# A gated delta-rule layer on one Trainium2 core: the triangular inverse kept in 32x32 blocks, a pipeline one turn deeper, three projection banks in rotation, a new order of steps

## The reference

```python
q = silu(conv4(x @ Wq)); k = silu(conv4(x @ Wk)) * 128**-0.5; v = silu(conv4(x @ Wv))
alpha, beta = sigmoid(x @ Wa + ba), sigmoid(x @ Wb + bb)
def step(S, (qt, kt, vt, at, bt)):               # for each of 2048 tokens, S is 128x128
    err = S @ kt - vt
    S = at * S - bt * outer(err, kt)
    return S, S @ qt
out = x + (layernorm(o) * ln_w + ln_b) * sigmoid(x @ Wg) @ Wo + experts
```

## Time and profile before

| | |
|---|---|
| median of 3 runs | 4384.37 us (4383.68 to 4387.27) |
| profiled execution, its own time | 4386.71 us |
| its span | 4385.1 us |
| PE busy in the span | 4174.3 us, 95% |
| DVE busy | 3028.0 us, 69% |
| ACT, POOL busy | 46%, 41% |
| granted TensorE clock, mean | 0.99 |

### The profile page before, as it was taken

How to read it: one execution, slowest core, us unless ns; L and a number is a source line. 1 busy time by engine, 2 the same in 40 slices (tenths; PEclk the granted TensorE clock), 3 DMA queues, 4 the chain that set the end, 5 groups by cost and what they waited for, 6 DMA issues and landing times. The chain is left out here.

```text
span 4385.1 us, 94472 instructions
## 1 busy us (share of the span) xinstructions
PE 4174.3 (95%) x28800; PEld 3435.8 (78%) x28800; DVE 3028.0 (69%) x7067; ACT 2033.0 (46%) x4992; POOL 1805.5 (41%) x3109
## 2 busy tenths in 40 slices
PE   8999799999999999999999999999999999996999
PEld 6777688888888788888888888888888888885887
DVE  4444577777777777777777777777777777774222
ACT  3433355555555555555555555555555555553111
POOL 3444444444444444444444444444444444441000
PEclk9999899999999999999999999999999999997999
DMA  3333411111111111111221111111111111113453
GB/s 128 131 139 139 151 38 40 39 39 39 39 41 39 39 39 39 39 39 39 77 77 39 39 39 40 40 39 39 40 39 39 39 39 39 39 27 104 147 145 114
DMA packets 371455, 270.27 MB, mean 62 GB/s; under 512 B 153456, under 2 KB 284528, under 8 KB 369360
## 3 DMA queue, kind: packets, MB, share of 16 engines
q1 hardware_dynamic: 368848, 261.29, 21.0%
q0 software_dynamic: 2560, 8.39, 0.5%
HBM read 209.85 MB, written 59.77 MB: 61 GB/s over the span
## 5 line engine op out<-in xcount | busy, mean ns | idle before, releaser
L1247 PE MATMUL bank<-hx_hi,w_hi 128*128 128x512 f32 x2048 | 927.4, 453 | 136.6 <-DVE conv L1052 110.1
L1247 PE MATMUL bank<-hx_lo,w_hi 128*128 128x512 f32 x2048 | 907.8, 443 | 0.0
L1247 PE MATMUL bank<-hx_hi,w_lo 128*128 128x512 f32 x2048 | 895.0, 437 | 0.0
L1052 DVE SCALAR_TENSOR_TENSOR conv<-bank,tap,conv 128x512 f32<-128x512 f32 x1152 | 848.7, 737 | 15.7 <-ACT conv L1190 6.4
L1247 PEld LDWEIGHTS bank<-hx_hi,w_hi 128*128 128x128 f32 x2048 | 390.6, 191 | 200.2 <-issue 82.4
L921 POOL TENSOR_TENSOR masked<-LT,mask 128x256 f32<-128x256 f32 x512 | 412.9, 837 | 190.8 <-DVE LT L1070 190.7
L1008 DVE SCALAR_TENSOR_TENSOR S<-S,gamma,bank 128x128 f32<-128x128 f32 x480 | 164.7, 343 | 449.5 <-PE bank L1333 447.2
L940 POOL TENSOR_TENSOR oG<-oT,gT 128x512 f32<-128x512 f32 x128 | 166.0, 1297 | 709.1 <-ACT oT L1208 709.1
L1247 PEld LDWEIGHTS bank<-hx_hi,w_lo 128*128 128x128 f32 x2048 | 390.0, 190 | 75.4 <-issue 43.8
L897 POOL TENSOR_TENSOR prods<-Lb,Tc 128x28 f32<-128x28 f32 (+6 forms) x896 | 204.0, 228 | 504.1 <-ACT Lb L1176 441.8
L1136 ACT ACTIVATE MT<-bank 128x256 f32<-128x256 f32 x512 | 196.3, 383 | 457.3 <-PE bank L1270 457.2
(11 more groups left out here) (147 smaller groups left out, 9529.6 us busy)
## 6 DMA issues: line engine op xcount, KB each, us to landing
gamma<-gamma_d SPq DMA_DIRECT2D x128, 258.0 KB, 3.2
alpha<-alpha_d SPq DMA_DIRECT2D x128, 256.0 KB, 3.6
oT_d<-oG SPq DMA_DIRECT2D x128, 256.0 KB, 2.4
o_raw<-oT_d SPq DMA_DIRECT2D x32, 1024.0 KB, 6.8
gu_raw<-in_gate_up SPq DMA_DIRECT2D x17, 1408.0 KB, 6.2
dn_raw<-in_down SPq DMA_DIRECT2D x17, 512.0 KB, 4.6
x_in<-in_x SPq DMA_DIRECT2D x8, 1024.0 KB, 9.3
w_raw<-in_Wk SPq DMA_DIRECT2D x32, 256.0 KB, 3.1
```

Source lines behind the costliest of these rows:

```text
L1052: dve.scalar_tensor_tensor(out=conv[i][:, to], in0=PJ[i][:], scalar=tap[:, i, j + 1:j + 2], in1=conv[i][:, to], op0=ALU.mult, op1=ALU.add) ...
L1247: last = pe.matmul(dst, a[:, i, k], b[:, k, cols], start=(j == 0), stop=(j == 3 * KC - 1))
```

## The change

The inverse up to 32x32 is held in compact form: `TTb` and `Tnb` keep, for each chunk, the four diagonal 32x32 blocks as 128 partitions x 32 columns. The merges to 16 and 32 become matmuls of 32x32 diagonal blocks (16 in each of four visits); the product is not masked beforehand on POOL, but afterwards on DVE, which writes `Yb` (new L1045) in place of ACT's copy `MT`. After the second level ACT puts the blocks in place in `TT` (L1169) and in `Tn64` (L1175). `diag` and `Lc` work on the diagonal blocks alone.

The inverse is split over two turns: `inv` (group g+2) does the two small levels, `late` (group g+1) the merges to 64 and 128, `AT`, and the rows of k and v. `proj` moves to group g+3, and there is one more turn ahead of the first full one. At four places of a turn (`VISIT_AT`) PE does the blocks of both groups behind each other, 16 of `inv`, then 8 or 4 of `late`. `AT`'s matmuls and DVE's `AT` are one piece instead of two. The projections rotate over banks 0, 1 and 2 (`PJ_OF`), with the wait for each looked up in `PJ_FREED`. A turn has 38 steps where it had 19, and all tables are new.

```diff
+TB = 32
 LEVELS = [8, 16]
-STEPS = 19
-CHAIN = {1: 0, 2: 1, 4: 2, 5: 3, 7: 4, 8: 5, 10: 6, 11: 7, 13: 8, 14: 9, 16: 10, 17: 11}
...
-MT_AT = {6: 0, 9: 1}
-TT_AT = {7: 0, 10: 1}
-Y32_AT, T32_AT, Y64_AT, T64_AT = 13, 14, 16, 17
...
+PJ_OF = [[0, 1, 2, 0], [1, 2, 0, 1], [2, 0, 1, 2], [0, 1, 2, 1]]
+PJ_FREED = [[(1, 0), (1, 3), (1, 2), (0, 0)], [(1, 1), (1, 2), (1, 3), (0, 0)],
+            [(1, 1), (1, 2), (1, 3), (0, 0)], [(1, 1), (1, 2), (1, 3), (0, 1)]]
...
+VISIT_AT = {9: 0, 15: 1, 28: 2, 34: 3}
...
+YB_AT = {11: 0, 28: 1}
+TT_AT = {19: 0, 31: 1}
...
+PLACE_AT = {8: (0, 1), 7: (2, 3)}
...
+        TTb = sb("TTb", [P, 2, G, TB])
+        Tnb = sb("Tnb", [P, 2, G, TB])
+        Yb = sb("Yb", [P, G, TB])
+        Tn64 = sb("Tn64", [2 * TB, G, 2 * TB])
+        MT = sb("MT", [P, G, 2 * TB])
+        TT = sb("TT", [P, 2, G, C])
...
-        masked = sb("masked", [P, len(LEVELS), G, C])
-        TT = sb("TT", [P, 2, G, C])
-        Tn = sb("Tn", [P, G, C])
...
-        PJ, IB, TR, CO = (bank[0], bank[1], bank[2], bank[1]), bank[3:5], bank[5], bank[6:8]
+        PJ, WL, WH, TR, CO = bank[0:3], bank[3], bank[4], bank[5], bank[6:8]
...
-            turn(eng, -1, 2, False, False, True, False)
-            turn(eng, -1, 3, False, True, True, False)
+            turn(eng, -1, 1, False, False, False, True, False)
+            turn(eng, -1, 2, False, False, True, True, False)
+            turn(eng, -1, 3, False, True, True, True, False)
             for g in range(GROUPS):
-                turn(eng, 0, g, True, True, True, g > 0)
+                turn(eng, 0, g, True, True, True, True, g > 0)
             with nc.Fori(1, NH - 1, engines=bass.OrderedEngineSet([eng.engine]), hint_back_edge=True) as hh:
                 for g in range(GROUPS):
-                    turn(eng, hh, g, True, True, True, True)
+                    turn(eng, hh, g, True, True, True, True, True)
             for g in range(GROUPS):
-                turn(eng, NH - 1, g, True, g < 3, g < 2, True)
-            turn(eng, NH, 0, False, False, False, True)
+                turn(eng, NH - 1, g, True, g < 3, g < 2, g < 1, True)
...
-                    if inv and s == 1:
-                        pool.wait_ge(solve_done, at(SOLVE_PER, 2))
-                        wait(pool, chain_done, at(12, 0))
-                        pool.tensor_tensor(TT[:, (g + 1) % 2].rearrange("p c (q t) -> p c q t", t=SB),
-                                           Tc[:].rearrange("p c (o t) -> p c o t", o=1).to_broadcast([P, G, P // SB, SB]),
-                                           same[:].rearrange("p (c q t) -> p c q t", c=1, t=SB)
-                                           .to_broadcast([P, G, P // SB, SB]), ALU.mult).then_inc(t8_done, 1)
-                    if proj and s in MASK_AT:
-                        lvl = MASK_AT[s]
-                        pool.wait_ge(lt_done, at(1, 3))
-                        for c in range(2):
-                            wait(pool, step_done[c], at(STEP_PER, 1, 2 * lvl + 2))
-                            pool.tensor_tensor(masked[:, lvl, half(c)], LT[:, g % 2, half(c)], mask[lvl][:], ALU.mult)\
-                                .then_inc(mask_done, 1)
...
+                    if inv and s == T8P_AT:
+                        pool.wait_ge(solve_done, at(SOLVE_PER, 3))
+                        wait(pool, late_done, at(LATE_PER, 1))
+                        wait(pool, placed, at(4, 1))
+                        pool.tensor_tensor(TTb[:, cur].rearrange("p c (q t) -> p c q t", t=SB),
+                                           Tc[:].rearrange("p c (o t) -> p c o t", o=1).to_broadcast([P, G, TB // SB, SB]),
+                                           same_c[:].rearrange("p (c q t) -> p c q t", c=1, t=SB)
+                                           .to_broadcast([P, G, TB // SB, SB]), ALU.mult).then_inc(t8_done, 1)
...
+                    if inv and s in YB_AT:
+                        l = YB_AT[s]
+                        dve.wait_ge(step_done, at(4, 2, 2 * l + 1))
+                        dve.tensor_tensor(Yb[:], WL[:, 0:G * TB].rearrange("p (c t) -> p c t", c=G),
+                                          mask_c[:, l].rearrange("p (c t) -> p c t", c=1).to_broadcast([P, G, TB]),
+                                          ALU.mult).then_inc(yb_done, 1)
+                    if inv and s in TT_AT:
+                        l = TT_AT[s]
+                        dve.wait_ge(step_done, at(4, 2, 2 * l + 2))
+                        dve.tensor_tensor(TTb[:, cur], TTb[:, cur], WL[:, 0:G * TB].rearrange("p (c t) -> p c t", c=G),
+                                          ALU.subtract).then_inc(tt_done, 1)
+                        dve.wait_ge(tt_done, at(2, 2, l + 1))
+                        dve.transpose(Tnb[:, cur], TTb[:, cur]).then_inc(tn_done, 1)
...
-                    if inv and s in TT_AT:
-                        lvl = TT_AT[s]
-                        for c in range(2):
-                            dve.wait_ge(step_done[c], at(STEP_PER, 1, 2 * lvl + 3))
-                            dve.tensor_tensor(TT[:, par, half(c)], TT[:, par, half(c)],
-                                              IB[c][:, 0:2 * C].rearrange("p (c t) -> p c t", c=2), ALU.subtract)\
-                               .then_inc(tt_done[c], 1)
-                        for c in range(2):
-                            dve.wait_ge(tt_done[c], at(len(LEVELS), 1, lvl + 1))
-                            dve.transpose(Tn[:, half(c)], TT[:, par, half(c)]).then_inc(tn_done[c], 1)
...
+                        wait(dve, lc_done, at(1, 3))
+                        for q in range(P // TB):
+                            dve.tensor_tensor(diag[quad(q)], LT[quad(q), (g + 3) % 4, :, quad(q)],
+                                              same_c[quad(q)].rearrange("p (c t) -> p c t", c=1).to_broadcast([TB, G, TB]),
+                                              ALU.mult).then_inc(diag_done, 1)
...
-                    if inv and s in MT_AT:
-                        lvl = MT_AT[s]
-                        for c in range(2):
-                            act.wait_ge(step_done[c], at(STEP_PER, 1, 2 * lvl + 2))
-                            act.activation(MT[:, half(c)], IB[c][:, 0:2 * C].rearrange("p (c t) -> p c t", c=2),
...
+                    if late and s in PLACE_AT:
+                        act.wait_ge(tt_done, at(2, 2))
+                        wait(act, chain_done, at(12, 0))
+                        for q in PLACE_AT[s]:
+                            act.activation(TT[quad(q), par, :, quad(q)], TTb[quad(q), par], ACT.Copy).then_inc(placed, 1)
...
+                def bank_waits(i):
+                    back, user = PJ_FREED[ahead][i]
+                    if user == 3:
+                        wait(pe, tanh_done, at(1, 4 - back))
+                    else:
+                        wait(pe, conv_done, at(9, 3 - back, 3 * user + 3))
...
+                def visit(v):
+                    if inv:
+                        for c in range(G):
+                            for q in range(P // TB):
+                                w = WL[quad(q), c * TB:(c + 1) * TB]
+                                if v in (0, 2):
+                                    last = pe.matmul(w, LT[quad(q), (g + 2) % 4, c, quad(q)], Tnb[quad(q), cur, c],
+                                                     start=True, stop=True)
+                                else:
+                                    last = pe.matmul(w, Yb[quad(q), c], TTb[quad(q), cur, c], start=True, stop=True)
+                        last.then_inc(step_done, 1)
+                    if late:
+                        for c in range(G):
+                            if v in (0, 1):
+                                cols = slice(c * 64, c * 64 + TB)
+                                for u in (0, 2):
+                                    lo, hi = quad(u), quad(u + 1)
+                                    if v == 0:
+                                        last = pe.matmul(WH[hi, cols], LT[lo, (g + 1) % 4, c, hi], Tnb[lo, par, c],
+                                                         start=True, stop=True)
+                                    else:
+                                        last = pe.matmul(WH[lo, cols], MT[hi, c, 0:TB], TTb[hi, par, c],
+                                                         start=True, stop=True)
+                            if v == 2:
+                                last = pe.matmul(WH[64:128, c * 64:c * 64 + 64], LT[0:64, (g + 1) % 4, c, 64:128], Tn64[:, c],
+                                                 start=True, stop=True)
+                            if v == 3:
+                                last = pe.matmul(WH[0:64, c * 64:c * 64 + 64], MT[64:128, c], TT[64:128, par, c, 64:128],
+                                                 start=True, stop=True)
+                        last.then_inc(late_done, 1)
```

(44 more changed lines are left out.)

474 lines of the change are left out of this document (226 added, 248 removed).

## The result

The changed kernel takes 3937.35 us (median of 4, 3933.84 to 3940.71) against 4385.07 us before (median of 4): ratio 0.898, 95% interval [0.896, 0.899]. It is 448 us faster. The forecast was 4035 us, its range 3941 to 4153 us; the result lies just under the range, where the rival "cheaper still" (3929 us) stood.

A forecast was written before the change was run, and what follows sets the result against it. PE was taken to set the pace. A turn of 27.20 us less 1.84 (small levels) and 1.11 (wait) plus 0.10 (new waits) gave 24.35; with 13.1 filling and 20.6 emptying, 4035 us, range 3941 to 4153.

The forecast's parts named there:

- cheaper still: Rival: small instructions at 0.008 us, no price inside a visit, no new waits; turn 23.5 us, 3929 us; chance 0.11.
- filling and emptying: Before and after the full turns: 13.1 us more for filling, 20.6 us for one more emptying turn.
- 32 full-size instructions gone: Small levels on PE: 16 matmuls of 128x128 go, 32 instructions at 0.112 us, saving 3.58 us a turn.
- 128 small instructions: New diagonal blocks in four visits: 32 instructions each at 0.012 us, adding 1.54 us a turn.
- changes from 32x32 to 64x64: Block size changing inside visits 2 and 3: 0.1 us each, adding 0.20 us a turn.
- edges of the visits: Entering and leaving PE's four small-block visits: already paid in the old kernel, so 0.
- wait for the convolution: Fourth projection's wait on DVE's convolution goes with three banks: 1.11 us a turn saved.
- new waits (`Lx`): New PE waits: 0.10 us a turn, bounds 0 and 1, `Lx` ready; rival of about 1.1 us more, 4166 us, chance 0.17.
- rows 5: Old trace of 32x32 visits, two positions taking turns, 0.016 us an instruction; four were read as 0.008 or 0.016.
- DVE's tail at the turn's end: After visit 3: DVE's transpose, convolution piece and `S`, about 2.0 us, against 2.2 us of PE work.
- Dearer blocks: Rival: small blocks at 0.032 us an instruction, 2.56 us a turn more than taken; 4354 us; chance 0.07.
- The slow loop over visit 3: Rival: visit 3, DVE's work behind it and the next chain step set the pace; 4435 us; chance 0.04.

The follow-up runs named there:

- e1: Changed kernel with the small blocks' loops turned round, array position outside and chunk inside, so four blocks of one position follow each other: 4098.77 us.
- e11: Changed kernel with the chain's steps 3, 6 and 9 moved up by two steps, one projection behind the step whose copy they read: 4115.69 us.
- e8: Kernel before with rotating banks, second and third convolution multiply-adds over 64 of 512 columns, and the chain's step 3 a step later: 4249.57 us.
- e6: Kernel before with rotating banks and each convolution's second and third multiply-add over only 64 of 512 columns: 4259.13 us.
- e5: Kernel before with the rotation of the projection banks 0, 1 and 2 alone: 4326.0 us.
- e3: Changed kernel with the bank rotation alone undone, every group projecting into banks 0, 1, 2, 1: 3938.7 us.
- e7: Changed kernel with the matmul that spreads `Lx` one step later on PE: 3922.6 us.
- e12: Changed kernel with the matmul that spreads `Lx` one step later and DVE's `Lx` copy one step earlier, ahead of `Yb`: 3919.67 us.
- e9: Changed kernel with the sixteen 32x32 matmuls of every late visit replaced by four full-size ones, small levels left out: 4175.99 us.
- e2: Changed kernel with every small block multiplied twice, 128 more small instructions a turn: 4110.15 us.
- e4: Changed kernel with each visit cut in two, the late blocks coming a step after the small ones: 4036.74 us.

## Why the prediction was wrong

The direction and the bound (PE's own list) hold. So does the sum of filling and emptying, but by luck: it was to be 13.1 + 20.6 = 33.7 and is 17.6 + 3.2 + 12.55 = 33.4, the fill 8 us dearer and the emptying 8 us cheaper. The whole miss, 98 us, is the turn: 24.35 forecast, 23.56 measured, 0.79 us too much. Its terms, a turn, with the starts of PE's instructions averaged over 112 turns of each kernel:

| term | forecast | measured |
|---|---|---|
| 32 full-size instructions gone | -3.58 | -3.58 |
| 128 small instructions | +1.54 | +1.10 |
| changes from 32x32 to 64x64 | +0.20 | +0.21 |
| edges of the visits | 0 | +0.02 |
| wait for the convolution | -1.11 | -1.17 |
| late starts of the chain's matmuls | not counted | -0.40 |
| late starts ahead of the first 64x64 blocks | not counted | -0.18 |
| new waits (`Lx`) | +0.10 | +0.23 |
| end of a loop pass | not counted | +0.09 |
| sum | -2.85 | -3.68 |

The direct difference of the turns is -3.64 (27.20 to 23.56); 0.04 are not accounted for, about what rounding makes over so many starts.

- **Mis-sized: the small instruction.** "I take 0.012 (between the first two)": it is 0.0086 by the row of 28 instructions, near the lower of the two readings (each position as busy as in rows 5, four sharing), and e1 shows why: with one position after another the same instructions need 0.023, and four positions that take turns share the time down to that value. 0.44 us a turn, 55 us in all. Its sign of being wrong (small instructions more than 0.016 apart) did not come. The Trainium skill ("TensorE: Matmul & The Clock Gate", section "Wait — 56ns, not 53.3ns?") has a floor of some 25 ns between starts; the row here is at a third of it. The Trainium skill ("TensorEngine Tiling (Array Packing)", Gotcha 1) bars different row tiles from one bank at once. This isn't borne out here either: all four write bank 3, each its own partitions, and e1 shows that they overlap.
- **Left out: late starts.** "The chain ... stay[s]: 0." It did not. In every turn before, the `S` step of the second chunk began 0.23 late and its second pass 0.10, and the `R` step of the first chunk was late too, by 0.22 in one turn of four and hardly in the others: 0.40 us a turn in all, 50 us. The prediction read PE's waits, where there is one line, and not PEld's, where `S` and `R` stand with 25.3 us in 35 turns. The new order puts more work between, and no late start is left in the chain. e11 makes such starts (+1.43) and e8 takes one away. The trace of before bounded this term; the forecast could have held it. Another 0.18 a turn, 23 us, was lost before on the two projections ahead of the first 64x64 blocks, and is lost in e6 and e8 as well. No wait for an engine is listed for it and its cause stays open.
- **Right in size, wrong in cause: the convolution's wait.** It went, 1.17 for 1.11 (1.07 ahead of the projection, and 0.10 ahead of the blocks behind it, which start on time where the wait is gone). But "with three banks" is not why. The banks alone give 0.47 in the old order (e5) and nothing in the new one (e3); the new order puts the fourth projection where both waits, for the convolution and for `Tn`, are over.
- **New waits.** +0.10 was for DVE's tail at the turn's end, which stays hidden, as "PE has ... 2.2 us" said: no wait for `S` at the turn's start. "`Lx` is ready when PE wants it" was wrong: it costs 0.23 (0.16 ahead of the pass, 0.07 in it), and e7 gets about half of it back in the time.
- **Small blocks' edges and changes of size.** 0 and 0.1 each were taken, 0.02 in all and 0.10 each measured. The edge is easily mistaken for a late start:

```profile
2025.11 0.44 PE L1307 MATMUL bank<-TT,MT 32*32 32x32 f32 x16
2025.48 0.49 PE L1319 MATMUL bank<-S,kT 128*128 128x128 f32 x2
2025.72 0.48 PE L1247 MATMUL bank<-hx_lo,w_hi 128*128 128x512 f32 x1
```

Here, in the kernel before, two passes on `S` take 0.24 where 0.14 is normal. But DVE had written `S` by 2023.89. It is the 0.10 of leaving the blocks, which in the changed kernel the projection behind a visit pays.
- **The rivals.** "Cheaper still" came within 9 us (3929; its own terms without rounding, a turn of 23.54, give 3934). That is luck in part: it took the small instruction nearly right, but had nothing for the change of size, `Lx` and the loop's end (some 0.6 too little together with the 0.0006 an instruction), and nothing for the late starts and 0.06 of the wait (some 0.6 too much). Its chance of 0.11 was too low because the two readings of rows 5 were treated as ends, while the middle had no row of its own. "Dearer blocks" is beyond even what its own order of loops gives (e1, 4099 us for 4354). The slow loop over visit 3 is in no trace.

## What to carry to other kernels

Read the waits of the weight load beside those of the matmuls: where PE is 96% busy and one wait is listed, another 0.4 us of 27 stood there. A serial chain that runs between independent matmuls wants enough of them between a product and its reuse: here two 512-column matmuls lost 0.3 us, one lost 0.6 to 1.0, and three with a visit lost nothing. And many small matmuls should take turns over the row blocks of the array, and be put in one visit: 0.0086 us each instead of 0.023, and 0.2 us net for every visit that is saved. When a change removes a wait, try the named part alone: here the part that looked like the cause was worth 0.47 alone and nothing in company.

## What the runs showed that I had not expected

The end of each loop pass (four turns) costs PE time once the list is long. In a plain run projections are 0.23 apart; here the first row of the last pair starts 1.18 us behind its forerunner, in e12:

```profile
1113.30 0.40 PE L1284 MATMUL bank<-hx_hi,w_lo 128*128 128x512 f32 x1
1114.48 0.49 PE L1284 MATMUL bank<-hx_hi,w_hi 128*128 128x512 f32 x1 [0.79 <-DVE conv L1080]
```

The convolution named had ended at 1113.88 (1113.17 and 0.71 us), 0.60 before the start; the same place in the changed kernel once took 2.48:

```profile
1969.60 0.40 PE L1284 MATMUL bank<-hx_hi,w_lo 128*128 128x512 f32 x1
1972.08 0.50 PE L1284 MATMUL bank<-hx_hi,w_hi 128*128 128x512 f32 x1 [2.08 <-issue]
```

And the page's DMA queues (queue and kind: packets, MB, share of 16 engines), first of the kernel after, then of e9, whose loop holds 96 matmul instructions fewer a turn:

```profile
q8 instruction: 354, 5.80, 0.6%
```

```profile
q8 instruction: 25, 0.41, 0.0%
```

The changed kernel has 354 packets of instructions, the kernel before and e9 25. In the mean over passes the fourth turn is 0.34 us longer than its neighbours at this place in the changed kernel, 0.6 in e7, 0.84 in e12 and 1.27 in e2 (482 packets), and exactly as long as they in e9. With the same 354 packets and a slower PE it is 0.29 in e4 and only 0.10 in e1 and e11. So it grows as PE gets ahead, and with the length of the loop: e2 loses the most although its PE is as slow as in e1 (24.6 and 24.7 us for the other turns). That e9 loses nothing shows less, since its turn is the slowest of these (25.4 us). It is about 10 us of the 3937, and part of why e7 gains 15 us instead of 30: three turns of four became 0.2 to 0.3 us shorter, the fourth 0.05 longer, which makes 22 us in the profiled executions; the medians differ by 15. That the fetch itself is what PE waits for is an inference from this; no run changed the code's length alone.
